# Moving the transposes of one quarter's hidden rows, and the steps that feed them, within the end of a one-core transformer block

## What is computed

```python
# first block: conditioned attention and feed-forward
x1 = _ln(x) * (1.0 + scale1) + shift1          # shift, scale, gate: from the condition row of the batch
qkv = x1 @ qkv_w + qkv_b                       # 16 heads of 128
attn = softmax(q k^T / sqrt(128)) v            # within each batch entry, 32 tokens
x = x + gate1 * (attn_out @ out_w + out_b)
x2 = _ln(x) * (1.0 + scale2) + shift2
x = x + gate2 * (gelu(x2 @ ffn_w1 + ffn_b1) @ ffn_w2 + ffn_b2)
# second block: feed-forward with quantised rows and ternary weights
def _linear_bit(x, w, g):
    xq = _act_quant(_rmsnorm(x, g))            # per row: scale = 127 / max|.|, round, divide
    return einsum('bsd,od->bso', xq, _ternary_quant(w))
h = silu(_linear_bit(x, w1, g1)) * _linear_bit(x, w2, g2)      # 1024 hidden channels
out = x_in + _linear_bit(h, w3, g3)
```

## Time and profile before

| | us |
|---|---|
| median of 3 runs (322.38 to 323.32) | 322.68 |
| the profiled execution | 322.68 |
| its span | 320.5 |
| TensorE busy | 310.7 (97%) |
| VectorE busy | 224.0 (70%) |
| ScalarE busy | 183.3 (57%) |
| GpSimd busy | 124.8 (39%) |

### The profile page before, as it was taken

How to read it: one execution, slowest core, us unless ns; L and a number is a source line. 1 busy time by engine, 2 the same in 40 slices (tenths; PEclk the granted TensorE clock), 3 DMA queues, 4 the chain that set the end, 5 groups by cost and what they waited for, 6 DMA issues and landing times.

```text
span 320.5 us, 9863 instructions
## 1 busy us (share of the span) xinstructions
PE 310.7 (97%) x4197; PEld 276.9 (86%) x4197; DVE 224.0 (70%) x448; ACT 183.3 (57%) x356; POOL 124.8 (39%) x109
## 2 busy tenths in 40 slices
PE   8999999999999999999999999999999999999986
PEld 7879989899998989888898997779998879998665
DVE  4747985955995985606568139879368688995996
ACT  2747383555435474556433926587536677468793
POOL 2338304100940893565420522146430244315591
PEclk9999999999999999999999999999999999999999
DMA  7991990410039343120020000200020200200011
GB/s 232 299 357 58 285 338 7 141 27 2 2 98 233 106 130 133 36 66 2 5 66 4 0 18 17 69 2 2 2 68 0 68 4 2 68 0 2 0 35 65
DMA packets 21026, 24.41 MB, mean 76 GB/s; under 512 B 1972, under 2 KB 18520, under 8 KB 20984
## 3 DMA queue, kind: packets, MB, share of 16 engines
q1 hardware_dynamic: 20608, 23.50, 24.2%
q10 hardware_dynamic: 376, 0.30, 0.3%
HBM read 22.68 MB, written 1.11 MB: 74 GB/s over the span
## 4 chain that ended last, share of the span: by engine, by line
PE 80%; DVE 7%; ACT 5%; issue 4%; DMA 2%; SPq 1%; POOL 0%; ACTq 0%; DVEq 0%
PE proj_banks L580 34%; PE out_bank L580 17%; PE wide_banks L580 5%; PE proj_banks L643 4%; PE turn_bank L580 4%; PE att_banks L673 3%; PE wide_banks L865 3%; DMA stage<-in_L_cond_qkv_w 2%; PE att_banks L580 2%; PE wide_banks L673 1%; ACT work L1898 1%; PE att_banks L865 1%; PE wide_banks L748 1%; PE proj_banks L865 1%; ACT L1757 1%
## 5 line engine op out<-in xcount | busy, mean ns | idle before, releaser
L1764 ACT ACTIVATE q_t<-proj_banks,bias_cols 128x256 f32<-128x256 f32 x64 | 30.3, 474 | 48.3 <-PE proj_banks L580 48.0
L580 PE MATMUL proj_banks<-x_hi,w_hi 128*128 128x256 f32 x252 | 53.2, 292 | 0.6 <-ACT k_t L1764 0.5
L580 PE MATMUL proj_banks<-x_lo,w_hi 128*128 128x256 f32 x252 | 49.8, 279 | 0.0
L580 PE MATMUL proj_banks<-x_hi,w_lo 128*128 128x256 f32 x252 | 49.7, 279 | 0.0
L580 PEld LDWEIGHTS proj_banks<-x_hi,w_hi 128*128 128x128 f32 x252 | 38.7, 189 | 4.5 <-issue 1.8
L580 PEld LDWEIGHTS proj_banks<-x_lo,w_hi 128*128 128x128 f32 x252 | 38.5, 189 | 0.0
L580 PEld LDWEIGHTS proj_banks<-x_hi,w_lo 128*128 128x128 f32 x252 | 38.3, 188 | 0.0
L1260 DVE TENSOR_TENSOR v_sb<-proj_banks,bv_row 128x512 f32<-128x512 f32 x32 | 21.7, 683 | 23.0 <-PE proj_banks L580 13.7
L1764 ACT ACTIVATE k_t<-proj_banks,bias_cols 128x256 f32<-128x256 f32 x64 | 30.0, 468 | 0.0
L580 PE MATMUL out_bank<-wo_hi,at_hi 128*128 128x256 f32 x128 | 21.6, 291 | 0.5
L2108 POOL TENSOR_TENSOR w_lo<-stage,w_hi 128x1024 fp32r<-128x1024 f32 x6 | 14.3, 2392 | 19.9 <-DVE w_hi L1215 14.2
(11 more groups left out here) (327 smaller groups left out, 780.7 us busy)
## 6 DMA issues: line engine op xcount, KB each, us to landing
stage<-in_L_cond_qkv_w SPq DMA_DIRECT2D x16, 256.0 KB, 4.7
...
```

The lines of the kernel that those rows point to most:

```text
L580: mm = pe.matmul(dst, l, r, start=start and i == 0, stop=stop and i == len(seq) - 1)
L1764: act.activation(dst[:, h, :], proj_bank[h % 2][:, s * QT:(s + 1) * QT], ACT.Identity, bias=bias_cols[:, c:c + 1]).then_inc(qk_kept, 1)
```

## The change

No instruction's work is changed; steps move on four engines, and two waits are written anew.

- TensorE: `attend(NU - 1)` stands one `ffn1` tile earlier and the sixth tile behind the last `out_proj`. `hq_turn(a - 1, 1, h_tiles[1])` leaves its place in front of `ffn1(b, ...)` and stands behind `end_z(1)`, in front of `end_ffn2(b, 2)`, with a wait for `q_kept` of `q_turn(a, 0)`, which uses the same bank; `q_turn(a, 0)` waits for one `hq_kept` less, and the last products wait for it.
- VectorE: of `h_tiles[0]` the maximum comes behind the last attention's `at_low`, and its `hidden_deq` right behind its rounding. Of `h_tiles[1]` the maximum, the rounding and `hidden_deq` all come behind `h_low(b, 3)`. In `end_quantise(a)` the step `first` is `h_low(b, 0)` and `between` is `h_low(b, 1)`.
- ScalarE: `keep_hq(a - 1, 1)` goes from in front of `gelu(b, 0)` to behind `end_silu(1)`; the square of tile 1 goes from in front of `gelu(b, 1)` to behind `h_high(b, 0)`.
- GpSimd: the roots of quarter 2 are made for each tile by itself.

```diff
--- before.py
+++ after.py
@@ -838,7 +838,7 @@
                     pe.wait_ge(q_rounded, 2 * (2 * b + t + 1))
                 pe.wait_ge(ffn2_read, b + 1)
                 if b == NQ - 2 and t == 0:
-                    pe.wait_ge(hq_kept, 2 * b)
+                    pe.wait_ge(hq_kept, 2 * b - 1)
                 if t == 1 and free:
                     pe.wait_ge(gelu_done, MT * (NQ - 1))
                 elif alone:
@@ -1025,11 +1025,12 @@
             a, b = NQ - 2, NQ - 1
             out_proj(NU - 2, 1)
             pe.wait_ge(at_lo_made, 2 * (NU - 1))
-            ffn1(a, range(0, 3))
+            ffn1(a, range(0, 2))
             attend(NU - 1)
-            ffn1(a, range(3, 6))
+            ffn1(a, range(2, 5))
             for t in range(2):
                 out_proj(NU - 1, t)
+            ffn1(a, range(5, 6))
             hq_turn(a - 1, 0, h_tiles[0])
             ffn1(a, range(6, MT))
             for t in range(2):
@@ -1040,7 +1041,6 @@
             for j in (2, 3):
                 for t in range(2):
                     late_ffn2(a, t, j)
-            hq_turn(a - 1, 1, h_tiles[1])
             ffn1(b, range(MT), end_ffn1_bank, True)
             end_ffn2(b, 0)
             q_turn(a, 0, turn_bank, late_xg)
@@ -1048,10 +1048,13 @@
             q_turn(a, 1, wide_bank[1], late_xg, free=True)
             end_z(0)
             end_z(1)
+            pe.wait_ge(q_kept, 2 * a + 1)
+            hq_turn(a - 1, 1, h_tiles[1])
             end_ffn2(b, 2)
             end_ffn2(b, 3)
             end_z(2)
             end_z(3)
+            pe.wait_ge(hq_kept, 2 * a)
             for t in range(2):
                 last_product(a - 1, t, turn_bank, slice(t * D, (t + 1) * D), hqt_bf[a - 1][t])
             pe.wait_ge(xc_ready, NQ)
@@ -1517,6 +1520,7 @@
             def hidden_round(b, t, maximum):
                 ffn_after(steps.up(hidden_scales(b, t, maximum)))
                 dve.tensor_scalar(h_tiles[t], h_tiles[t], hqscale[:, b % 2, t:t + 1], ROUND, ALU.mult, ALU.add).then_inc(hq_rounded, 1)
+                hidden_deq(b, t)
 
             def output(b, t, src):
                 tile = xin[:, 2 * b + t, :]
@@ -1639,28 +1643,22 @@
                     x2_low(b, b + 1)
                 keep_v(u, 1)
                 softmax_shift(u)
+                if u == NU - 1:
+                    softmax_norm(u)
+                if u == NU - 1:
+                    for p in range(2):
+                        at_turn(u, p)
+                    for p in range(2):
+                        at_low(u, p)
+                if a >= 0:
+                    dve.wait_ge(g_weighed, 2 * a + 1)
+                    hidden_round(a, 0, hidden_max(a, 0, h_tiles[0]))
                 if u < NU - 1:
-                    if a >= 0:
-                        dve.wait_ge(g_weighed, 2 * a + 1)
-                        hidden_round(a, 0, hidden_max(a, 0, h_tiles[0]))
-                        hidden_deq(a, 0)
                     softmax_norm(u)
                     if a >= 0:
                         dve.wait_ge(g_weighed, 2 * a + 2)
                         hidden_round(a, 1, hidden_max(a, 1, h_tiles[1]))
-                        hidden_deq(a, 1)
                         outputs(a)
-                else:
-                    softmax_norm(u)
-                    dve.wait_ge(g_weighed, 2 * a + 1)
-                    maximum = hidden_max(a, 0, h_tiles[0])
-                    for p in range(2):
-                        at_turn(u, p)
-                    for p in range(2):
-                        at_low(u, p)
-                    hidden_round(a, 0, maximum)
-                    dve.wait_ge(g_weighed, 2 * a + 2)
-                    maximum = hidden_max(a, 1, h_tiles[1])
 
 
             a, b = NQ - 2, NQ - 1
@@ -1672,16 +1670,16 @@
 
             residual(b, late_xa)
             residual_stats(b, late_xa)
-            hidden_round(a - 1, 1, maximum)
             x2_norm(b, late_xa)
             h_low(a, 2)
             h_low(a, 3)
             end_x2_scale(b)
-            hidden_deq(a - 1, 0)
             ffn_residual(a, proj_bank[0])
-            end_quantise(a, xa, late_xg[:, :, :, :], lambda: hidden_deq(a - 1, 1), lambda: h_low(b, 0))
-            for j in range(1, MT // 2):
+            end_quantise(a, xa, late_xg[:, :, :, :], lambda: h_low(b, 0), lambda: h_low(b, 1))
+            for j in range(2, MT // 2):
                 h_low(b, j)
+            dve.wait_ge(g_weighed, 2 * a)
+            hidden_round(a - 1, 1, hidden_max(a - 1, 1, h_tiles[1]))
             half = [slice(i * MC, (i + 1) * MC) for i in range(2)]
 
             def scale_last(t, inverse):
@@ -2021,12 +2019,11 @@
 
 
             a, b = NQ - 2, NQ - 1
-            keep_hq(a - 1, 1, hqt_bf[a - 1][1])
             gelu(b, 0, end_ffn1_bank)
-            for t in range(2):
-                square(a, t)
+            square(a, 0)
             gelu(b, 1, end_ffn1_bank)
             h_high(b, 0)
+            square(a, 1)
             gelu(b, 2, end_ffn1_bank)
             h_high(b, 1)
             gelu(b, 3, end_ffn1_bank)
@@ -2054,6 +2051,7 @@
             keep_q(a, 1, wide_bank[1])
             end_silu(0)
             end_silu(1)
+            keep_hq(a - 1, 1, hqt_bf[a - 1][1])
             square_hidden(a, 0, late_h, 6)
             end_silu(2)
             square(b, 0, late_xa, 5)
@@ -2248,7 +2246,8 @@
                 pool.tensor_tensor(dst[:, cols], h[:, cols], g3_row[:, cols], ALU.mult).then_inc(h_weighted, 1)
 
             x2_rstd(b)
-            rms_of_both(a)
+            rms_of(a, 0)
+            rms_of(a, 1)
             pool.wait_ge(h_lo_dve, 6)
             gate_bias(b, gate1, late_gb)
             ffn_bias(b, late_xa, late_gb)
```

## The result

The changed kernel takes 324.73 us, the median of 19 runs (323.83 to 326.15); the kernel before, run beside it, 322.52 us (322.07 to 324.47, 19 runs). The ratio is 1.0069, with a 95% interval of 1.0057 to 1.0082: 2.2 us slower, in an interval from 1.8 to 2.6. The forecast of 324.2 had the sign and the range. As a time it was 0.5 us short, and as a difference 0.7 us (forecast 1.5, measured 2.2).

The account below looks back on a forecast made before the run. TensorE, busy 97% of the span, was taken as the bound. A lead of 0.24 us, a new wait of 1.3 and 0.43 for the transposes made `end_ffn2(b, 2)` 1.5 us late: 322.68 to 324.2 us, range 322.9 to 325.2.

Parts of the forecast that it names:

- Step 1: At `attend(NU - 1)`, one tile earlier: TensorE waits 0.34 us for the transposed probabilities, bounds 0.2 and 0.5.
- Step 2: Around `ffn1(b)`: transposes taken from in front (0.43 us) and two hitches gone (0.15) leave TensorE at -0.24 us.
- Step 3: Before the transposes of `h_odd`: TensorE waits 1.3 us for VectorE's rounding; `end_ffn2(b, 2)` 1.5 us late.
- Step 5: GpSimd beside VectorE's maximum and rounding of `h_odd`: rounding taken undisturbed at 0.76 us, a doubling only for the upper bound.
- The doubled rounding: VectorE's rounding of `h_odd` beside GpSimd: 0.76 us more on the wait, 2.3 us in all, as upper bound.
- the second rival: Rounding of `h_odd` doubled by contention, or a late root making `q_turn(a, 0)` wait: 325.0 us; chance 0.12.
- The exchange one for one: At the hand-over to the tail: whatever delays `end_ffn2(b, 3)` delays `q_turn(b, 0)` and the end by as much.
- Step 4: Moved VectorE steps (2.9 us) and `keep_hq` stay hidden; VectorE idled 1.97 us before `end_hidden(0)`, 1.12 before `last_gate`.
- Ready in time: Rounding of `h_odd` ready when TensorE reaches its transposes, so no wait there: +0.2 us, 322.9 us; chance 0.2, lesser waits included.
- The clock: TensorE's clock halves in the new 1.3 us gap, doubling the 3.0 us from 293.18: about 327.2 us; chance 0.02.

Follow-up runs that it names:

- e8: Changed kernel with both squares of quarter 2 back in front of the second pair of GELUs; 324.94 us, ratio 1.0078.
- e2: Changed kernel with GpSimd's `gate_bias(b)` and `ffn_bias` waiting until the rounding of `h_odd` is over; 324.52 us, ratio 1.0060.
- e9: Changed kernel with GpSimd's `gate_bias(b)` moved in front of `rms_of(a, 0)`, beside VectorE's maximum of `late_xg`; 325.20 us, ratio 1.0074.
- e11: As e9 on the changed kernel, but `gate_bias(b)` starts 2 us earlier still, after VectorE's last `x_lo` of quarter 3; 324.23 us, ratio 1.0043.
- e5: Changed kernel with one more VectorE maximum of `h_odd`, result unused, in front of its own; 325.50 us, ratio 1.0095.
- e3: Changed kernel with the transposes of `h_odd` between `end_ffn2(b, 2)` and `end_ffn2(b, 3)`; 324.46 us, ratio 1.0060.
- e10: As e9 on the changed kernel, with the transposes of `h_odd` also between `end_ffn2(b, 2)` and `end_ffn2(b, 3)`; 324.58 us, ratio 1.0057.
- e4: Changed kernel with the last attention and the sixth `ffn1(a)` tile back at their old places; 324.88 us, ratio 1.0075.
- e1: Changed kernel with the maximum of `h_odd` behind the last attention and its rounding before `x2_norm`, as before; 323.45 us, ratio 1.0023.

## Why the prediction was right, and where it was short

**Step 1, the attention.** Forecast a new wait of 0.34 us, between 0.2 and 0.5; measured 0.37.

**Step 2, TensorE's lead.** Forecast -0.24 us; measured -0.34 at `end_z(1)`: +30.20, which is the row of 293.67 above, against +30.54 before, which is this row:

```profile
292.51 1.03 PE L865 MATMUL att_banks<-w12t,qt_bf 128*128 128x512 fp8e4 x4
```

`ffn1(b)` and the first two `end_ffn2` ran without the hitches. Right, 0.1 us short.

**Step 3, when the rows are ready.** Forecast in the clock of the profile before: the scale at 288.3, the maximum when the last `h_low` is over, at 291.7. Measured +26.13, which is 288.10, and +29.57, which is 291.54. Both right within 0.2 us. The forecast also had VectorE (291.1) and ScalarE's last `h_high` (291.0) come to the last `h_low` at the same moment, and e8 bears that out: with VectorE earlier, ScalarE holds it up. The way through maximum, reciprocal and scale was as summed. Up to here the chain of steps held.

**Step 5, the neighbour, is the term that failed in size.** Step 5 of the prediction took the rounding as undisturbed, at 0.76 us, and it took 1.57. TensorE reached the place at +30.87 (0.67 behind `end_z(1)`, as before the change), and started at +33.01: a loss of 2.14 us where I had 1.3. Of the 0.8 us between, 0.81 is the rounding, and the small rest (0.1 of lead, 0.1 of earlier readiness) cancels. With 0.41 for the transposes and -0.34 of lead that is 2.21 at `end_ffn2(b, 2)`, forecast 1.5. The doubled rounding was in the text as a bound, with the price 2.3 us and 325.0 us and, as part of the second rival, a chance of 0.12; the time of 324.73 lies nearer to that rival than to the forecast. Four kernels show the cause by taking it away, and the rounding reads 0.75 us in each: e2 holds GpSimd back, e9 and e11 send it ahead, e5 sends VectorE later.

Could it have been read from the profile before? Yes, and better than as a doubling. GpSimd's operation beside the product of the earlier trace rows is

```profile
308.63 1.27 POOL L2248 TENSOR_TENSOR late_weighted<-work,g_row 128x512 f32<-128x512 f32 x1
```

and ends at 309.90; the product ends at 310.44, 0.54 us later. So what that row priced was not a factor of two but the rest of the neighbour's time. For the other kind of instruction, which I called unpriced, there was a row too, on GpSimd's side:

```profile
272.45 1.59 POOL L2167 TENSOR_TENSOR h_lo<-work,h_hi 128x512 fp32r<-128x512 f32 x1 [2.16 <-ACT h_hi L1851]
```

It takes 1.29 us elsewhere and began while VectorE's rounding of the even rows (272.13, 0.75 us) was running; it lost 0.30 us. So a rounding with a single tensor input does hold up GpSimd's difference, and the reverse was to be feared. With that, the overlap could be worked out, in hindsight: `late_gb` starts some 0.15 us behind the last `h_low`, `late_gb` and `late_xa` last 2.6 us, and the rounding wants to begin 1.74 us behind the same point. It would stand for 1.0 us and then take 0.55: an estimate of 1.55 us instead of 0.76, and 325.0 us in all.

**The exchange one for one.** I wrote that whatever delays `end_ffn2(b, 3)` delays the end by as much. For the change it held: 2.21 us at `end_ffn2(b, 2)`, 2.07 at `q_turn(b, 0)`, 2.09 at the last half product, 2.2 in the time. As a general rule it failed in e2, e3 and e10, where TensorE came sooner and VectorE's own path, disturbed by GpSimd, ended last: 0.77, 0.56 and 0.53 us of idle TensorE at `q_turn(b, 0)`.

**Step 4, what was hidden** stayed hidden. VectorE still idles 2.01 us before `last_gate`, and `keep_hq` holds nothing up. What step 1 had wrong, without harm to the sum, was that "nothing comes of" the new place of the even rows' maximum. It makes their rounding start 0.95 us later (+11.11 against +10.16), which costs nothing in the changed kernel (it ends at +12.02, and TensorE comes to these rows at +12.45); in e4 it held TensorE up, and in e1 it delayed `xt`.

**The rivals.** *Ready in time* would have needed the maximum 1.1 us sooner (291.54 against 290.4); e1, where the rows were ready, shows what it would have given: no idle time at the transposes. *The clock* did not fall in this kernel and did in e5.
